# Weight pieces in self attention: the copies move to both ends of the row exponentials, the subtractions in among the row maxima

## The chip, the cores and the metric

One core of one Trainium2 chip runs the kernel. The metric is the device time of one execution in microseconds (us), smaller is better; the figure before is the median of three runs. Engines are named TensorE (PE; PEld is its weight load), VectorE (DVE), ScalarE (ACT), GpSimd (POOL) and SyncE (SP), which issues most of the transfers.

## The reference

A decoder layer on x of 4 x 512 x 512 numbers in fp32: causal self attention with 16 heads of 32 and rotary positions, cross attention to a masked context of 1601 rows, and a mixture of 16 experts (4 per token) beside a shared one, each followed by a residual and a layer norm.

```python
q, k, v = (proj(Wq), proj(Wk), proj(Wv))
q = q * cos + _rotate_half(q) * sin
k = k * cos + _rotate_half(k) * sin
att = jnp.einsum('bhqd,bhkd->bhqk', q, k) / math.sqrt(hd)
att = jax.nn.softmax(att + mask, axis=-1)
out = jnp.einsum('bhqk,bhkd->bhqd', att, v)
...
x = _layernorm(x + _L0_attn_ref(x, L0_attn_Wq, L0_attn_Wk, L0_attn_Wv, L0_attn_Wo), axis=-1)
x = _layernorm(x + _L0_xattn_ref(x, ctx_2048, mask_BxS2_bk0), axis=-1)
x = _layernorm(x + _L0_ffn_ref(x, ...), axis=-1)
```

## The kernel before

Products are made to fp32 accuracy from two parts of each operand: a high part in the multiplier's own format (fp32r) and the low rest, x - high. Three products of parts replace one. So every operand is split once: ScalarE copies it (the rounding copy is the high part), and VectorE or GpSimd subtracts that copy from the value.

Self attention (`self_attention`) works in 16 groups, numbered g = 0 to 15: four batches b of 512 rows, in each four groups hg of four heads. The engines run their own instruction streams and wait on semaphores. One group, in the order of TensorE's stream (`group` under `block.tensor`):

- Stage A: 16 tiles of row scores, n = 0 to 15 (L546, mask L548), in pairs, and between the pairs 40 of the 48 projection products (L506) of the next group. VectorE takes each tile's row maximum (L456), ScalarE its row exponentials with their sum (L331). A tile lies in one of three PSUM buffers, so the score of tile n waits for the exponential of tile n - 3. In groups with hg = 0, except the first, the output projection of the batch before (L525) and its residual follow.
- The row maxima are turned (L630), and ScalarE (L347) and VectorE (L471) copy them below q.
- Stage B: transposed scores (L562), their exponentials (L355) on ScalarE, the causal zeroing of diagonal blocks by GpSimd (`hide_later`, L263), and the products with v (L569). VectorE rotates q and k of the next group meanwhile (L391 to L409), ScalarE rounds q (`hi_q`, L303) and GpSimd takes its rest (`lo_q`, L252). GpSimd does `lo_q` behind the zeroing of the third block column, of four. `turn_heads` (L599) then transposes the heads of the next group, which waits for q's rest, the roped k and v; ScalarE (L323) and VectorE (L446) copy the result out, and the next group's scores begin.

Beside this, self attention splits the first 24 pieces of the experts' weights for the last part of the kernel. A piece is 128 x 512 numbers. It is fetched into one of two slots in a part of the buffer `rows` that is free till the end of the stage (`fetch`, L202), rounded by ScalarE (`hi_piece`, L314), its rest taken in place by VectorE (`lo_piece`, L427), and both parts are stored to memory (`store`, L207). A slot's fetch waits until the store of its piece before has landed. Groups 1 to 12 do two pieces each: k = 2(g - 1) and the next. Before the change ScalarE copies them behind the row exponentials n = 2 and n = 4, VectorE subtracts them both at the end of its part of the group, behind the copy of the turned inverses (`keep_inverse`, L417), and SyncE stores both and then fetches the next two. SyncE's stream also holds the loads of the next batch's x (`load_x`, L212).

Other work in the stages: in groups with hg = 3 ScalarE splits two blocks of x behind n = 1 and 3 (`hi_x`, L292), in groups with hg = 2 two behind n = 9 and 11, and GpSimd takes their rests (L247). Behind n = 6 ScalarE rounds the output of the group before (`hi_out`, L310), and GpSimd takes its rest (`lo_out`, L256). VectorE scales that output behind n = 3 (`finish_out`, L423).

Of the kernel before, what the change touches and what calls it, by code (L numbers as in the profile page):

```python
# [59 lines left out]
NF = 2  # L60
FIRST_GROUPS = range(1, 1 + FIRST * WE // FIRST_PIECE // NF)
# [12 lines left out]
def self_attention(nc, sem, rows, xT, x, wqkvT, woT, rope, w_experts, w_split, split_steps, gather_x1):  # L74
# [3 lines left out]
    with ExitStack() as ctx:  # L78
# [57 lines left out]
        def row_place(n):  # L136
            return score_ps[:, n % 3, :] if n % 3 < 2 else den_ps[:, :]
# [8 lines left out]
        def w_places(c):  # L146
            return staged[:, c * HG * GW:(c + 1) * HG * GW], wqkv[:, 0, c, :], wqkv[:, 1, c, :]

        def wo_places():
            return staged[:, DC * HG * GW:], *(wo[:, part, :, :].rearrange("p g n -> p (g n)") for part in range(2))  # L150
# [4 lines left out]
        def piece_place(k, part):  # L155

            at = (k % NF * 2 + part) * FIRST_PIECE
            return spare[:, at:at + FIRST_PIECE]

        def pieces_of(g):  # L160
            return range((g - 1) * NF, g * NF) if g in FIRST_GROUPS else range(0)

# [22 lines left out]
        with nc.Block() as block:  # L185

            @block.sync
            def _(sp):
                for c in range(DC):
                    sp.dma_start(x_raw[:, c, :], xT[0, :, c, :]).then_inc(chunk_in[c], 16)  # L190
                    sp.dma_start(w_places(c)[0], wqkvT[:, c, :]).then_inc(chunk_in[c], 16)
                sp.dma_start(cos_t[:, :, :], rope[0]).then_inc(tables_in, 16)
                sp.dma_start(sin_t[:, :, :], rope[1]).then_inc(tables_in, 16)
                sp.dma_start(wo_places()[0], woT).then_inc(wo_in, 16)
                def in_memory(k):
                    expert, at = k // (WE // FIRST_PIECE), k % (WE // FIRST_PIECE) * FIRST_PIECE
                    return w_experts[1 + expert, :, at:at + FIRST_PIECE], w_split[expert, :, :, at:at + FIRST_PIECE]

                def fetch(k):
                    if k >= NF:  # L200
                        sp.wait_ge(piece_out[k % NF], 16 * (k // NF))
                    sp.dma_start(piece_place(k, 1), in_memory(k)[0]).then_inc(piece_in[k % NF], 16)  # L202

                def store(k):
                    sp.wait_ge(piece_lo, k + 1)
                    at = k % NF * 2 * FIRST_PIECE
                    sp.dma_start(in_memory(k)[1], spare[:, at:at + 2 * FIRST_PIECE].rearrange("p (a n) -> p a n", a=2)  # L207
                                 ).then_inc(piece_out[k % NF], 16)

                def load_x(b):  # L210
                    sp.wait_ge(x_lo, b * TT)
                    sp.dma_start(x_raw[:, :, :], xT[b]).then_inc(x_in, 16)  # L212

                load_x(1)
                sp.wait_ge(w_lo, DC + 1)
                for k in range(NF):
                    fetch(k)
                sp.dma_start(rows[:, 0:NT - TT, :], x[:, 0:NT - TT, :]).then_inc(rows_in, 16)
                for g in FIRST_GROUPS:
                    if g % HG == 0 and g // HG + 1 < B:  # L220
                        load_x(g // HG + 1)
                    for k in pieces_of(g):
                        store(k)
                    for k in pieces_of(g + 1):
                        fetch(k)
                assert (B - 2) * HG in FIRST_GROUPS
                for slot in range(NF):
                    sp.wait_ge(piece_out[slot], 16 * len(FIRST_GROUPS))
                sp.dma_start(rows[:, NT - TT:NT, :], x[:, NT - TT:NT, :]).then_inc(rows_in, 16)
# [56 lines left out]
            def _(act):  # L286
# [25 lines left out]
                def hi_piece(k):  # L312
                    act.wait_ge(piece_in[k % NF], 16 * (k // NF + 1))
                    nc.scalar.activation(piece_place(k, 0).bitcast(F32R), piece_place(k, 1), ACT.Copy  # L314
                                         ).then_inc(piece_hi, 1)

                def group(b, hg, first, last):
                    g = b * HG + hg

                    act.wait_ge(scored_t, g * NS)  # L320
                    for h in range(GH):
                        act.wait_ge(turned, g * 2 * GH + 2 * h + 1)
                        nc.scalar.activation(q_st[0:3 * HD, h, :], proj_ps[0:3 * HD, 2 * h % 4, :],  # L323
                                             ACT.Copy).then_inc(q_stacked, 1)
                    for n in range(NS):
                        qt, h = n // GH, n % GH
                        w = (qt + 1) * P
                        act.wait_ge(maxed, g * NS + n + 1)
                        if n == 0:
                            act.wait_ge(inverted, g)  # L330
                        nc.scalar.activation(row_place(n)[:, 0:w], row_place(n)[:, 0:w], ACT.Exp,  # L331
                                             bias=neg_row_max[:, qt, h:h + 1], accum_out=row_sum[:, qt, h:h + 1]
                                             ).then_inc(row_exped, 1)
                        if n in (1, 3) and hg == HG - 1 and not last:
                            hi_x(b + 1, 2 + n // 2)
                        if n in (2, 4) and g in FIRST_GROUPS:
                            hi_piece(pieces_of(g)[n // 2 - 1])
                        if n == 6 and not first:
                            hi_out(g - 1, (hg - 1) % HG)
                        if n == 7 and g == 0:  # L340
                            hi_wo()
                        if n in (9, 11) and hg == HG - 2 and b < B - 1:
                            hi_x(b + 1, n // 2 - 4)

                    act.wait_ge(max_turned, g + 1)
                    for h in range(0, GH, 2):
                        nc.scalar.activation(q_st[3 * HD:P, h, :], den_ps[32 * h:32 * h + 32, :],  # L347
                                             ACT.Copy).then_inc(max_stacked_a, 1)
                    act.wait_ge(summed, g)
                    for kc in range(TT):  # L350
                        w = T - kc * P
                        for h in range(GH):
                            n = kc * GH + h
                            act.wait_ge(scored_t, g * NS + n + 1)
                            nc.scalar.activation(p_t[:, h, p_at[kc]:p_at[kc] + w],  # L355
                                                 score_ps[:, n % 2, kc * P:T], ACT.Exp).then_inc(exped, 1)
                            if n == 2 * GH + 1 and not last:
                                hi_q(g + 1)
# [11 lines left out]
            def _(dve):  # L370
# [48 lines left out]
                def finish_out(g):  # L419

                    dve.wait_ge(summed, g + 1)
                    dve.wait_ge(inv_kept, g + 1)
                    nc.vector.tensor_tensor(o_f[:, :], o_ps[:, :], o_f[:, :], ALU.mult).then_inc(o_scaled, 1)  # L423

                def lo_piece(k):
                    dve.wait_ge(piece_hi, k + 1)
                    nc.vector.tensor_tensor(piece_place(k, 1).bitcast(F32R), piece_place(k, 1), piece_place(k, 0),  # L427
                                            ALU.subtract).then_inc(piece_lo, 1)
# [11 lines left out]
                def group(b, hg, first, last):  # L440
                    g = b * HG + hg
# [7 lines left out]
                    for qt in range(TT):  # L449
                        for h in range(GH):  # L450
                            n = qt * GH + h
                            dve.wait_ge(scored, g * NS + n + 1)
                            if n == 0:
                                dve.wait_ge(max_lo, g)
                                dve.wait_ge(row_exped, g * NS)
                            nc.vector.tensor_reduce(neg_row_max[:, qt, h:h + 1], row_place(n)[:, 0:(qt + 1) * P],  # L456
                                                    AX, ALU.max, negate=True).then_inc(maxed, 1)
                            if n == 3 and not first:
                                finish_out(g - 1)
                    dve.wait_ge(maxed, g * NS + NS)  # L460
                    dve.wait_ge(max_turned, g)
                    nc.vector.tensor_copy(neg_max[:, :, :, 0], neg_row_max[:, :, :]).then_inc(max_hi, 1)
# [15 lines left out]
                    keep_inverse(g)  # L478
                    if g == 0:
                        lo_w(DC, wo_places())  # L480
                    for k in pieces_of(g):
                        lo_piece(k)

                dve.wait_ge(tables_in, 32)
                rotate(0)
# [1685 lines left out]
```

## Time and profile before

| | |
|---|---|
| median of 3 runs | 1492.63 us (1491.56 to 1495.46) |
| the profiled execution | 1484.37 us, span 1482.7 us, mean granted clock 0.947 |
| busy, TensorE / its weight loads | 1312.1 us (88%) / 1041.5 us (70%) |
| busy, VectorE / ScalarE / GpSimd | 839.9 (57%) / 709.2 (48%) / 390.8 (26%) us |
| self attention | about the first 520 us of the span |
| zeroing of diagonal blocks, L263, 256 times | 95.8 us busy |

The profile is of one execution, with every instruction's start and duration. A row of the timeline gives start, duration, engine, line of kernel.py, operation, written and read tensors and their shape; "xN" are N instructions merged; in brackets stand the engine's idle time just before and what ended it. Instructions of one engine can overlap a little, since the next is started before the last has drained.

### The profile page before, as it was taken

How to read it: one execution, taken by the hardware profiler on the slowest of the kernel's cores; microseconds unless marked ns; L12 is line 12 of the kernel's file. 1: busy time of each engine (PE TensorE's matmuls, PEld its weight loads, DVE VectorE, ACT ScalarE, POOL GpSimd, SP SyncE). 2: the span in 40 equal slices, each digit the busy share in tenths (PEclk: the TensorE clock that was granted, in tenths of full speed). 3: DMA queues.
4: the chain of work that ended last, by engine and by line, in shares of the span. 5: the costliest groups of instructions: out<-in, count | busy, mean ns of one | idle time of the engine just before them, and what ended most of it. 6: DMA issues, size and time to landing. Idle time of an engine off the chain costs nothing. (4 is left out here: it accounts for less than half of the span.)

```text
span 1482.7 us, 22215 instructions
## 1 busy us (share of the span) xinstructions
PE 1312.1 (88%) x7473; PEld 1041.5 (70%) x7473; DVE 839.9 (57%) x1764; ACT 709.2 (48%) x1589; POOL 390.8 (26%) x491
## 2 busy tenths in 40 slices
PE   5899999999999858999899997896999999899960
PEld 4666676666676447888788786785788887788850
DVE  6777677676766556665666655684333333233316
ACT  4777577577747624444344533422333333233323
POOL 0234223234322320100101000102454553555420
PEclk9999999999999879999999999998999999999985
DMA  4212111112110035677667574416888999985657
GB/s 184 100 44 89 54 58 43 72 44 84 46 57 1 1 129 195 214 241 264 221 224 256 186 252 147 187 61 241 287 200 269 272 229 316 276 205 109 108 92 298
DMA packets 96907, 235.59 MB, mean 159 GB/s; under 512 B 10584, under 2 KB 47452, under 8 KB 93856
## 3 DMA queue, kind: packets, MB, share of 16 engines
q1 hardware_dynamic: 78960, 188.96, 36.4%
q0 software_dynamic: 17840, 45.22, 14.8%
q8 instruction: 65, 1.06, 0.3%
q14 instruction: 42, 0.34, 0.1%
HBM read 146.20 MB, written 87.95 MB: 158 GB/s over the span
## 5 line engine op out<-in xcount | busy, mean ns | idle before, releaser
L1993 PE MATMUL e_both_ps<-e_w,e_x_t 128*128 x948 | 243.8, 406 | 9.3 <-DMA e_w<-w_split 9.3
L1993 PEld LDWEIGHTS e_both_ps<-e_w,e_x_t 128*128 128x128 f32 x948 | 174.6, 191 | 46.4 <-issue 9.7
L506 PE MATMUL proj_ps<-wqkv,x_sp 128*128 128x384 f32 x768 | 172.1, 354 | 10.8 <-DVE wqkv L378 10.8
L1860 POOL DMA_INDIRECT acc_rows<-e_y,token_row x79 | 125.4, 1587 | 174.7 <-ACT e_y L1904 85.6
L1173 PE MATMUL c_score_ps<-ct,x_t 128*128 128x402 f32 x768 | 160.8, 363 | 0.0
L263 POOL TENSOR_SCALAR_AFFINE_SELECT p_t<-p_t 128x128 f32<-128x128 f32 x256 | 95.8, 387 | 218.8 <-ACT p_t L355 215.0
L1196 PE MATMUL c_out_ps<-cr,weigh_t 128*128 128x512 f32 (+1 forms) x624 | 149.8, 397 | 1.4 <-DVE weigh_t L1014 1.4
L1173 PEld LDWEIGHTS c_score_ps<-ct,x_t 128*128 128x128 f32 x768 | 142.8, 196 | 5.6 <-issue 4.5
L506 PEld LDWEIGHTS proj_ps<-wqkv,x_sp 128*128 128x128 f32 x768 | 130.5, 193 | 12.6 <-issue 11.0
L1929 DVE TENSOR_TENSOR e_x_t<-e_turn_ps,e_x_t 128x512 fp32r<-128x512 f32 x79 | 54.6, 692 | 147.0 <-ACT e_x_t L1891 131.8
L1196 PEld LDWEIGHTS c_out_ps<-cr,weigh_t 128*128 128x128 f32 (+1 forms) x624 | 115.8, 188 | 28.7 <-issue 1.7
L2016 PE MATMUL e_down_ps<-e_w,e_h_t 128*128 x474 | 124.8, 398 | 7.1 <-DVE e_h_t L1941 7.1
L355 ACT ACTIVATE p_t<-score_ps 128x512 f32<-128x512 f32 (+3 forms) x256 | 101.7, 436 | 57.1 <-PE score_ps L562 54.0
L2016 PEld LDWEIGHTS e_down_ps<-e_w,e_h_t 128*128 128x128 f32 x474 | 89.4, 189 | 29.9 <-issue 8.6
L1897 ACT ACTIVATE e_gated<-e_both_ps 128x256 f32<-128x256 f32 x79 | 30.4, 385 | 166.5 <-PE e_both_ps L1993 162.5
L1851 POOL DMA_INDIRECT e_x_g<-x_rows,token_row x79 | 80.0, 1013 | 103.0 <-DVE token_row L1578 61.4
L1936 DVE TENSOR_TENSOR e_h_f<-e_both_ps,e_gated 128x256 f32<-128x256 f32 x79 | 33.5, 424 | 125.3 <-ACT e_gated L1897 123.9
L331 ACT ACTIVATE score_ps<-score_ps,neg_row_max 128x128 f32<-128x128 f32 (+3 forms) x176 | 87.3, 496 | 28.5 <-DVE neg_row_max L456 27.4
L456 DVE TENSOR_REDUCE neg_row_max<-score_ps 128x1 f32<-128x128 f32 (+3 forms) x176 | 82.6, 483 | 31.7 <-PE score_ps L548 30.1
L1904 ACT ACTIVATE e_y<-e_down_ps,e_weight 128x512 f32<-128x512 f32 x79 | 54.3, 688 | 95.2 <-PE e_down_ps L2016 81.1
L562 PE MATMUL score_ps<-q_st,k_st 128*128 128x256 f32 (+2 forms) x256 | 87.2, 400 | 13.7 <-ACT p_t L355 12.7
L562 PEld LDWEIGHTS score_ps<-q_st,k_st 128*128 128x128 f32 x256 | 43.3, 194 | 74.0 <-ACT p_t L355 48.8
(233 smaller groups left out, 2267.2 us busy)
## 6 DMA issues: line engine op xcount, KB each, us to landing
e_w<-w_split SPq DMA_DIRECT2D x15, 3072.0 KB, 12.1
w_split<-c_piece SPq DMA_DIRECT2D x96, 384.0 KB, 3.6
c_piece<-w_experts SPq DMA_DIRECT2D x96, 192.0 KB, 3.7
raw<-ctxT SPq DMA_DIRECT2D x16, 800.5 KB, 4.4
w_split<-rows SPq DMA_DIRECT2D x24, 512.0 KB, 3.5
raw<-ctx_rows SPq DMA_DIRECT2D x16, 768.0 KB, 5.3
acc_rows<-rows SPq DMA_DIRECT2D x8, 1024.0 KB, 12.0
rows<-w_experts SPq DMA_DIRECT2D x24, 256.0 KB, 2.8
```

The source lines that it names most:

```text
L263: nc.gpsimd.affine_select(out=block_of, in_=block_of, compare_op=ALU.is_ge, fill=0.0, base=0, pattern=[[1, P]], channel_multiplier=-1).the ...
L331: nc.scalar.activation(row_place(n)[:, 0:w], row_place(n)[:, 0:w], ACT.Exp, bias=neg_row_max[:, qt, h:h + 1], accum_out=row_sum[:, qt, h:h ...
L355: nc.scalar.activation(p_t[:, h, p_at[kc]:p_at[kc] + w], score_ps[:, n % 2, kc * P:T], ACT.Exp).then_inc(exped, 1)
L456: nc.vector.tensor_reduce(neg_row_max[:, qt, h:h + 1], row_place(n)[:, 0:(qt + 1) * P], AX, ALU.max, negate=True).then_inc(maxed, 1)
L506: mm = nc.tensor.matmul(proj_ps[:, tt, 0:GW], x_sp[:, xs, c, tt * P:(tt + 1) * P], wqkv[:, ws, c, hg * GW:(hg + 1) * GW], start=(c == 0 an ...
L562: nc.tensor.matmul(score_ps[:, n % 2, q0:T], k_st[:, h, kc * P:(kc + 1) * P], q_st[:, h, q0:T], start=True, stop=True).then_inc(scored_t, 1)
L1173: mm = nc.tensor.matmul(score_ps[:, f, 0:MQ], x1_t[:, xs, c, n % XR * P:(n % XR + 1) * P], ct[:, cs, c, f * MQ:(f + 1) * MQ], start=(late ...
L1196: mm = nc.tensor.matmul(out_ps[:, n % 2, :], weigh_t[0:k, ws, c, :], cr[0:k, cs, c, :], start=(c == 0 and m == 0), stop=(c == MC - 1 and m ...
L1851: nc.gpsimd.indirect_dma_start(x_g[:, m % XG, :], None, x2_rows, bass.IndirectOffsetOnAxis(ap=token_row[:, 0, m:m + 1], axis=0)).then_inc( ...
L1860: nc.gpsimd.indirect_dma_start(acc[m % 2], bass.IndirectOffsetOnAxis(ap=token_row[:, 1, m:m + 1], axis=0), y[:, m % YB, :], None, compute_ ...
L1993: mm = nc.tensor.matmul(both_ps[:, m % 2, :], x_t[:, m % 2, xs, c * P:(c + 1) * P], weights(slot, ws, c * GU, (c + 1) * GU), start=(c == 0 ...
L2016: mm = nc.tensor.matmul(down_ps[:, m % 2, :], h_t[:, m % 2, hs, i * P:(i + 1) * P], weights(slot, ws, DOWN + i * D, DOWN + (i + 1) * D), s ...
```

## The change

The first of a group's two pieces is rounded ahead of the first row exponential, the second behind the last. The rest of the first is taken behind the seventh row maximum (n = 6) of the same group, the rest of the second behind the second maximum (n = 1) of the next group. SyncE stores and fetches slot by slot. Nothing is computed otherwise.

```diff
@@ sync
                     for k in pieces_of(g):
                         store(k)
-                    for k in pieces_of(g + 1):
-                        fetch(k)
+                        if k + NF < n_pieces:
+                            fetch(k + NF)
@@ scalar, group
+                    for k in pieces_of(g)[0:1]:
+                        hi_piece(k)
                     for n in range(NS):
...
-                        if n in (2, 4) and g in FIRST_GROUPS:
-                            hi_piece(pieces_of(g)[n // 2 - 1])
...
+                    for k in pieces_of(g)[1:2]:
+                        hi_piece(k)
                     act.wait_ge(max_turned, g + 1)
@@ vector, group
+                            if n == 1:
+                                for k in pieces_of(g - 1)[1:2]:
+                                    lo_piece(k)
                             if n == 3 and not first:
                                 finish_out(g - 1)
+                            if n == 6:
+                                for k in pieces_of(g)[0:1]:
+                                    lo_piece(k)
...
-                    for k in pieces_of(g):
-                        lo_piece(k)
```

VectorE, from the end of group 2 into group 3, before:

```order
L409 TENSOR_TENSOR qk_sp<-qk_cos,qk_sp 128x16x32
L417 COPY o_f<-den_ps 128x512
L427 TENSOR_TENSOR rows<-rows 128x512 x2
L446 CAST k_st<-proj_ps 96x512 x4
L456 TENSOR_REDUCE neg_row_max<-score_ps 128x1 x2
L456 TENSOR_REDUCE neg_row_max<-den_ps 128x1
L456 TENSOR_REDUCE neg_row_max<-score_ps 128x1
L423 TENSOR_TENSOR o_f<-o_ps,o_f 128x512
L456 TENSOR_REDUCE neg_row_max<-score_ps 128x1
L456 TENSOR_REDUCE neg_row_max<-den_ps 128x1
L456 TENSOR_REDUCE neg_row_max<-score_ps 128x1 x2
```

The same stretch after the change (the subtraction is now L431, the maxima L460, the copy of k L450):

```order
L413 TENSOR_TENSOR qk_sp<-qk_cos,qk_sp 128x16x32
L421 COPY o_f<-den_ps 128x512
L450 CAST k_st<-proj_ps 96x512 x4
L460 TENSOR_REDUCE neg_row_max<-score_ps 128x1 x2
L431 TENSOR_TENSOR rows<-rows 128x512
L460 TENSOR_REDUCE neg_row_max<-den_ps 128x1
L460 TENSOR_REDUCE neg_row_max<-score_ps 128x1
L427 TENSOR_TENSOR o_f<-o_ps,o_f 128x512
L460 TENSOR_REDUCE neg_row_max<-score_ps 128x1
L460 TENSOR_REDUCE neg_row_max<-den_ps 128x1
L460 TENSOR_REDUCE neg_row_max<-score_ps 128x1
L431 TENSOR_TENSOR rows<-rows 128x512
```

The two subtractions have left the place behind the copy of the inverses and stand singly behind the second and the seventh maximum.

ScalarE, around the first row exponentials of group 1, before:

```order
L323 ACTIVATE q_st<-proj_ps 96x512 x4
L331 ACTIVATE score_ps,row_sum<-score_ps,neg_row_max 128x128 x2
L331 ACTIVATE den_ps,row_sum<-den_ps,neg_row_max 128x128
L314 ACTIVATE rows<-rows 128x512
L331 ACTIVATE score_ps,row_sum<-score_ps,neg_row_max 128x128
L331 ACTIVATE score_ps,row_sum<-score_ps,neg_row_max 128x256
L314 ACTIVATE rows<-rows 128x512
L331 ACTIVATE den_ps,row_sum<-den_ps,neg_row_max 128x256
```

And after the change (the piece's copy is L316, the exponentials L335):

```order
L325 ACTIVATE q_st<-proj_ps 96x512 x4
L316 ACTIVATE rows<-rows 128x512
L335 ACTIVATE score_ps,row_sum<-score_ps,neg_row_max 128x128 x2
L335 ACTIVATE den_ps,row_sum<-den_ps,neg_row_max 128x128
L335 ACTIVATE score_ps,row_sum<-score_ps,neg_row_max 128x128
L335 ACTIVATE score_ps,row_sum<-score_ps,neg_row_max 128x256
```

The first copy stands ahead of all exponentials; the second has moved out of this stretch, behind the last one and ahead of L351, the copy of the turned maxima.

## Rows read from the trace of the kernel before

**Rows 1.** The page: the span, and the engines' busy time.

```profile
span 1482.7 us, 22215 instructions
...
PE 1312.1 (88%) x7473; PEld 1041.5 (70%) x7473; DVE 839.9 (57%) x1764; ACT 709.2 (48%) x1589; POOL 390.8 (26%) x491
```

**Rows 2.** The timeline, stage B of group 2, some of its rows.

```profile
102.91 0.50 PE L630 MATMUL den_ps<-ident_r,neg_max 128*128 128x128 f32 x4
...
112.17 1.37 DVE L427 TENSOR_TENSOR rows<-rows 128x512 fp32r<-128x512 f32 x2
...
112.47 1.23 POOL L263 TENSOR_SCALAR_AFFINE_SELECT p_t<-p_t 128x128 f32<-128x128 f32 x2 [0.67 <-ACT p_t L355]
...
113.67 1.28 POOL L252 TENSOR_TENSOR qk_sp<-qk_cos,qk_sp 128x512 fp32r<-128x512 f32 x1
...
115.00 2.68 PE L599 MATMUL proj_ps<-ident_r,qk_sp 128*96 128x128 f32 x32 [0.17 <-POOL qk_sp L252]
...
115.86 2.54 DVE L446 CAST k_st<-proj_ps 96x512 fp32r<-96x512 f32 x4 [2.31 <-PE proj_ps L599]
...
117.96 0.39 PE L546 MATMUL score_ps<-k_st,q_st 96*128 96x256 f32 x1
```

**Rows 3.** The timeline, group 14, which has no pieces: first score to the next group's.

```profile
466.03 0.38 PE L546 MATMUL score_ps<-k_st,q_st 96*128 96x256 f32 x1
...
478.79 0.51 PE L630 MATMUL den_ps<-ident_r,neg_max 128*128 128x128 f32 x4
...
488.36 0.57 POOL L263 TENSOR_SCALAR_AFFINE_SELECT p_t<-p_t 128x128 f32<-128x128 f32 x2 [0.67 <-ACT p_t L355]
...
488.89 1.28 POOL L252 TENSOR_TENSOR qk_sp<-qk_cos,qk_sp 128x512 fp32r<-128x512 f32 x1
...
490.22 2.68 PE L599 MATMUL proj_ps<-ident_r,qk_sp 128*96 128x128 f32 x32 [0.17 <-POOL qk_sp L252]
...
493.19 0.38 PE L546 MATMUL score_ps<-k_st,q_st 96*128 96x256 f32 x1
```

**Rows 4.** The line L427: count, ns min/median/max, first and last start.

```profile
L427 DVE TENSOR_TENSOR rows<-rows x24: 674/724/772, 84.2 to 432.2; 128x512 fp32r<-128x512 f32 x24
```

**Rows 5.** The timeline of TensorE, ends of stage A in groups 1 and 3.

```profile
62.01 0.39 PE L546 MATMUL score_ps<-k_st,q_st 96*128 96x256 f32 x1
...
74.90 0.51 PE L630 MATMUL den_ps<-ident_r,neg_max 128*128 128x128 f32 x4
...
131.08 0.50 PE L630 MATMUL den_ps<-ident_r,neg_max 128*128 128x128 f32 x4
```

**Rows 6.** The timeline of VectorE, group 1: the third, seventh and eighth maximum.

```profile
63.89 0.29 DVE L456 TENSOR_REDUCE neg_row_max<-den_ps 128x1 f32<-128x128 f32 x1 [0.84 <-PE den_ps L548]
...
66.44 0.81 DVE L456 TENSOR_REDUCE neg_row_max<-score_ps 128x1 f32<-128x256 f32 x2 [0.43 <-PE score_ps L548]
```

**Rows 7.** The timeline of ScalarE, group 1: exponentials one and eight, a piece, the maxima.

```profile
62.84 0.34 ACT L331 ACTIVATE score_ps<-score_ps,neg_row_max 128x128 f32<-128x128 f32 x1 [0.74 <-DVE neg_row_max L456]
...
66.18 0.62 ACT L314 ACTIVATE rows<-rows 128x512 fp32r<-128x512 f32 x1
...
68.12 0.45 ACT L331 ACTIVATE score_ps<-score_ps,neg_row_max 128x256 f32<-128x256 f32 x1
...
75.45 1.20 ACT L347 ACTIVATE q_st<-den_ps 32x512 fp32r<-32x512 f32 x2 [0.69 <-PE den_ps L630]
```

**Rows 8.** The page's transfers: count, KB each, us from issue to landing.

```profile
w_split<-rows SPq DMA_DIRECT2D x24, 512.0 KB, 3.5
```

**Rows 9.** Busy time by window; the last numbers are granted clock, DMA share, GB/s.

```profile
143.30:146.70 3.40, 3.40 (x34) 3.26 (x33) 2.06 (x3) 2.17 (x5) 0.80 (x4) 0.50 0.79 270
```

**Rows 10.** The timeline of TensorE: the first score of group 4.

```profile
147.05 0.38 PE L546 MATMUL score_ps<-k_st,q_st 96*128 96x256 f32 x1
```

**Rows 11.** The timeline: VectorE beside L252 at the start, GpSimd in group 3.

```profile
24.41 1.75 DVE L398 TENSOR_TENSOR qk_cos<-qk_cos,qk_sin 128x512 f32<-128x512 f32 x1
...
122.09 1.28 POOL L247 TENSOR_TENSOR x_sp<-x_raw,x_sp 128x512 fp32r<-128x512 f32 x1 [0.61 <-ACT x_sp L292]
```

More of the change, by code:

```diff
@@ L158, in piece_place @@
             return spare[:, at:at + FIRST_PIECE]
+        n_pieces = NF * len(FIRST_GROUPS)
         def pieces_of(g):
```

## The prediction

> **What bounds the kernel now.** The page comes first: 1482.7 us of span, TensorE busy for 88% of it [rows 1]. The change touches only self attention, so the rest of the page is set aside, and the timeline of that stage is read group by group. Fourteen of its sixteen groups look alike. Stage A runs from the first row score (L546) to the transpose of the row maxima (L630); stage B from there to the next group's first row score. The other views needed are the timelines of VectorE, GpSimd and ScalarE around these marks.
>
> *Stage B.* In group 2 the transpose starts at 102.91 and the next group's first score at 117.96, 15.05 us later [rows 2]. The 32 turns of the heads (L599) cannot start before GpSimd has finished the low part of q (L252, 113.67 to 114.95); their row names it as releaser, and they start at 115.00. GpSimd is late because of the row before: two diagonal selects (L263) that take 1.23 us together, from 112.47, while VectorE runs the two piece subtractions (L427) from 112.17 for 1.37 us. Group 14 has no pieces [rows 3]: the same two selects take 0.57 us, L252 starts 10.10 us after the transpose and not 10.76, L599 11.43 and not 12.09, the next first score 14.40 and not 15.05. That is a control inside the trace: what differs there is the pair of pieces, and 0.65 us follows it. The subtractions are 24, two in each of groups 1 to 12, from 84.2 to 432.2 us [rows 4], and the slow pair of selects stands in each of these groups.
>
> *Stage A.* TensorE, VectorE and ScalarE form a ring: a score needs a free one of three buffers, a maximum needs its score, an exponential its maximum, and a score two places on needs that exponential. Group 1 with its pieces takes 74.90 - 62.01 = 12.89 us, group 14 without pieces 478.79 - 466.03 = 12.76 us [rows 2, 3, 5]. Group 3, where ScalarE also splits two blocks of x among its first four exponentials, takes 131.08 - 117.96 = 13.12 us [rows 2, 5]. So 1.24 us of piece work inside ScalarE's row exponentials costs 0.13 us of time, and 0.36 where the x splits are there too.
>
> **The change, part by part.**
>
> *The two subtractions leave the end of the group.* Twelve groups (1 to 12) issue two of them there. GpSimd's pair of selects falls back from 1.23 to 0.57 us, and L252, L599 and the next group come 0.65 us earlier: 12 x 0.65 = **7.8 us** gained, all on TensorE's path. Late next would be L252 itself behind its own selects; group 14 shows nothing else in the way. VectorE had 2.31 us of idle time before its next copy (L446) [rows 2], so its own saving there is worth nothing.
>
> *The second subtraction goes behind the second maximum of the next group.* VectorE idles 0.84 us there until the third score [rows 6]; one piece takes 0.72, at most 0.77 [rows 4]. It fits with some 0.1 us to spare. Cost 0; bound, if the slack is missed, a few hundredths per group.
>
> *The first subtraction goes behind the seventh maximum.* VectorE has no idle time between maxima seven and eight (0.81 us for both) [rows 6], so the eighth moves by 0.7 us: 66.44 + 0.42 + 0.72 + 0.42, about 67.95. Its exponential started at 68.12 in group 1 [rows 7], since ScalarE was behind with two pieces and the split of o; without the pieces ScalarE is free earlier, so this exponential starts near 68.0. The later maximum is paid for by ScalarE's lead. VectorE catches up where it now waits for the ninth score. Net: about 0.05 us faster than now.
>
> *ScalarE's first copy goes ahead of the first exponential.* ScalarE waits 0.74 us there for VectorE, and the copy (L314) takes 0.62 [rows 7]. Cost 0. The data must be there: pieces are fetched one at a time as their slot's store lands, 3.5 us after issue [rows 8]. The first slot is stored after the seventh maximum, more than 20 us before its next use; the second after the next group's second maximum, some 2 us into stage A, stored by 5.5 us, fetched (half the bytes, so at most another 3.5) by 9 us, and wanted at 12.7 (75.45 - 0.69 - 62.01).
>
> *ScalarE's second copy goes behind the last exponential.* ScalarE waits 0.69 us there for the transpose; 0.62 fits, with little to spare. TensorE's transpose waits for the last exponential, not for this copy. Cost 0, bound 0.1 us per group.
>
> *The DMA queue* alternates store and fetch instead of two and two. The transfers are the same 24 and 24. The loads of x for the next batch stand behind one more store and start some 10 us later in two groups; they are used two groups on. Cost 0.
>
> *Stage A in sum.* Bounded above by group 14's time in every group: 9 x 0.13 + 3 x 0.36 = 2.3 us gained. Bounded below by the piece behind the seventh maximum reaching TensorE whole: 12 x 0.72 = 8.6 us lost. I take the value near the upper bound, since ScalarE's lead covers the delay: 9 x 0.05 for groups like group 1, and 3 x 0.25 for groups 3, 7 and 11, which lose their backlog: **1.2 us** gained.
>
> *Sum:* 7.8 + 1.2 = 9.0 us. The profiled execution took 1484.37 us (span 1482.7), 8.3 us under the median 1492.63 of the runs shown; so I expect a span near 1473.7 and a median of 1492.63 - 9.0 = **1483.6 us**.
>
> **Clock.** TensorE's granted clock drops to half (1.2 GHz of its two levels, 2.4 and 1.2) during the turns of some groups, just after the stretch in which it waits for GpSimd [rows 9]. Group 3 is one; its stage B takes 147.05 - 131.08 = 15.97 us [rows 5, 10] against group 2's 15.05, so a drop costs 0.92 us. Among groups 1 to 12 seven have one (3, 5, 6, 7, 9, 10, 12). The waiting before the turns gets shorter, which should not bring more drops, but where they fall is not decided by this kernel alone: none would be another 6.4 us gained, all twelve 4.6 us lost. I leave seven in the sum and put this into the range.
>
> **A rule against the sum.** The rows show one engine standing still for the other: the pair of selects beside the pieces takes twice its usual time [rows 2, 3], and in the first group's start VectorE's L398, begun just behind L252, took 1.75 us [rows 11], some 1.0 more than the like subtractions of [rows 4]. The Trainium skill (SBUF — State Buffer, "SBUF: two separate sides") says that VectorE with two SBUF inputs and a GpSimd operation that reads SBUF exclude each other for a whole instruction, whichever starts first. The trace agrees in both directions. By that rule the moved subtraction can itself be blocked in stage A, by GpSimd's subtractions of 1.28 us; that is the first rival.
>
> **The rivals.**
>
> *1. The moved subtraction meets GpSimd's.* In group 3 the x subtraction (L247) starts at 122.09, 4.13 us after the first score [rows 2, 11]; the new piece would start at about 4.8. With ScalarE's piece gone, L247 starts some 0.5 us sooner and ends at about 4.9, so VectorE waits 0.1 us, in three groups only. At worst it waits L398's surplus of 1.0 us: 3 us, inside the range. GpSimd's split of o follows ScalarE's, which comes behind the seventh exponential, after the piece has ended (5.6 against 6.0). Were that one met in all twelve groups, 12 x 1.0 us come back: 1495.6 us, no change to be measured. Chance 0.04.
>
> *2. Nothing is freed.* Something else holds L599, and only stage A's 1.2 us is gained: 1491.4 us. For it: the turns also wait for roped k and for v. Against it: group 14, in full. Chance 0.04.
>
> *3. Slower: the ring of stage A takes both subtractions.* If neither the idle 0.84 us nor ScalarE's lead hides them, 12 x 1.44 = 17.3 us are added against 7.8 gained: 1492.6 + 9.5 = 1502.1 us. It decides from the point where more than 0.65 of the 1.44 us reach TensorE per group. For it: the last exponential ends the stage, and the ring is tight in its second half. Against it: 1.24 us on ScalarE cost only 0.13 in the same ring. Chance 0.03.
>
> *4. More: the clock.* With the shorter wait no turn falls to half clock: 9.0 + 6.4 gained, 1477.2 us. Chance 0.05.
>
> **How the numbers follow.** The forecast has 0.84. Its own range goes from 1483.6 - 1.1 (stage A at its bound) - 3.7 (four drops fewer) = 1478.8 to 1483.6 + 4.6 (five more) = 1488.2; rounded out, 1478.5 to 1488.5. Left out are rivals 1, 2 and 3 (0.11), rival 4 (0.05) and the forecast's tails (0.04). About 0.3% (4.5 us) is what a measurement of this kernel can tell from no change: faster is forecast and rival 4, 0.89; same is rivals 1 and 2, 0.08; slower 0.03.
>
> **What would show it.** Right: the two selects before L252 take about 0.57 us in all groups; L252 starts 10.1 us and the next first score 14.4 us after L630 where the clock is full; stage A takes 12.8 to 12.9 us, in group 3 too; no idle time of ScalarE on the fetched piece. Wrong: stage A over 13.1 us, with VectorE late at the ninth maximum and TensorE waiting for an exponential at the tenth to twelfth score; a piece subtraction of well over 0.77 us (blocked by GpSimd); L347 starting later than 0.55 us after L630; or L599 still at 12.1 us.

## The result, and the profile after

| | before | after |
|---|---|---|
| median of the runs | 1493.97 us (4 runs, 1491.56 to 1495.46) | 1472.51 us (4 runs, 1466.78 to 1475.8) |
| ratio, 95% interval | | 0.9849 (0.9815 to 0.9884) |
| the same comparison again, 6 runs of after, 23 of before | 1490.98 us | 1474.62 us, 0.9874 (0.9848 to 0.9901) |
| span of the profiled execution | 1482.7 us | 1474.1 us |

Faster, and by about twice the 9.0 us of the forecast: 18.8 us by the ratio of the second comparison (14.8 to 22.7). The ratio is not that of the two medians, which lie 21.5 us apart in the first comparison and 16.4 in the second. The spans of the two profiles differ by only 8.6 us, so where the time went has to be read by stage. The mark used from here on is a group's first row score. In the profile before, groups 1 and 15 begin at 62.01 and 493.19, 431.18 us apart; in the one after:

```profile
63.90 0.38 PE L554 MATMUL score_ps<-k_st,q_st 96*128 96x256 f32 x1
...
478.54 0.39 PE L554 MATMUL score_ps<-k_st,q_st 96*128 96x256 f32 x1
```

That is 414.64 us, **16.5 us less**. The rest of the difference lies where the change touches nothing. Group 1 begins 1.9 us later, though group 0 has no pieces; 0.7 of it is in stage B of group 0 (17.68 us, and 17.01 before), where the stretch at half clock is 6.8 us long and was 3.4. In the eleven other profiles of this study that mark lies between 61.96 and 64.34, and neither end belongs to one kernel: filler, with the old code in group 0, has 63.67, both_at_seven, with the new, 62.21. From group 15 to the end the profile before takes 989.5 us, the one after 995.6; the code there is the same in all kernels, and the thirteen profiles give 989.5 to 999.4. The profile before is the luckiest of them. 16.5 - 1.9 - 6.1 = 8.6.

**Stage B.** The timeline of group 2 after, rows that answer to [rows 2]; its transpose of the maxima starts at 103.79 (the maxima are now L460, the pieces' subtraction L431, their copy L316, the selects L265, q's rest L254, the turns L607):

```profile
103.79 0.43 PE L638 MATMUL den_ps<-ident_r,neg_max 128*128 128x128 f32 x3
...
113.35 0.57 POOL L265 TENSOR_SCALAR_AFFINE_SELECT p_t<-p_t 128x128 f32<-128x128 f32 x2 [0.66 <-ACT p_t L359]
...
113.89 1.28 POOL L254 TENSOR_TENSOR qk_sp<-qk_cos,qk_sp 128x512 fp32r<-128x512 f32 x1
...
115.22 2.67 PE L607 MATMUL proj_ps<-ident_r,qk_sp 128*96 128x128 f32 x32 [0.17 <-POOL qk_sp L254]
...
118.17 0.38 PE L554 MATMUL score_ps<-k_st,q_st 96*128 96x256 f32 x1
```

The pair of selects is back at 0.57 us; q's rest starts 10.10 us after the transpose, and the next group 14.38 us after it. Stage B reads 14.37 to 14.41 us in all groups from 1 to 13: each is what group 14 was before [rows 3].

**Stage A.** VectorE in group 3, after, to be read against [rows 6]:

```profile
118.66 0.54 DVE L460 TENSOR_REDUCE neg_row_max<-score_ps 128x1 f32<-128x128 f32 x2
119.12 0.68 DVE L431 TENSOR_TENSOR rows<-rows 128x512 fp32r<-128x512 f32 x1
120.03 0.29 DVE L460 TENSOR_REDUCE neg_row_max<-den_ps 128x1 f32<-128x128 f32 x1 [0.23 <-PE den_ps L556]
...
122.59 0.42 DVE L460 TENSOR_REDUCE neg_row_max<-score_ps 128x1 f32<-128x256 f32 x1 [0.44 <-PE score_ps L556]
122.93 0.68 DVE L431 TENSOR_TENSOR rows<-rows 128x512 fp32r<-128x512 f32 x1
123.53 0.42 DVE L460 TENSOR_REDUCE neg_row_max<-score_ps 128x1 f32<-128x256 f32 x1
```

One subtraction stands in the idle stretch before the third maximum, which has shrunk to 0.23 us from the 0.84 read in group 1 before; the other moves the eighth maximum to 123.53. ScalarE at the end of the same stage, against [rows 7]:

```profile
130.66 0.62 ACT L316 ACTIVATE rows<-rows 128x512 fp32r<-128x512 f32 x1
131.44 1.20 ACT L351 ACTIVATE q_st<-den_ps 32x512 fp32r<-32x512 f32 x2 [0.16 <-PE den_ps L638]
```

The copy fills the wait for the transpose, 0.16 us of it are left, and L351 starts 0.54 us after the transpose (130.90), as before. Stage A takes 12.74, 12.77, 12.73 and 24.04 us in groups 1 to 4, where it took 12.89, 12.95, 13.12 and 24.16: as little as in groups without pieces. Over the twelve groups that is 2.4 us.

**The clock.** Windows, one over each of groups 5 and 6. The columns are busy time and instructions of TensorE, its weight loads, VectorE, ScalarE and GpSimd; then granted clock, DMA share and GB/s. Before:

```profile
186.00:215.00 29.00, 27.04 (x205) 19.30 (x204) 20.85 (x40) 21.51 (x59) 8.55 (x18) 0.94 0.18 61
215.00:244.00 29.00, 27.27 (x204) 19.20 (x197) 20.57 (x39) 22.00 (x60) 11.14 (x20) 0.94 0.16 54
```

And after:

```profile
184.00:211.00 27.00, 25.64 (x197) 18.14 (x196) 20.16 (x39) 21.16 (x59) 7.87 (x18) 1.00 0.16 59
211.00:239.00 28.00, 26.73 (x203) 19.08 (x204) 21.04 (x42) 22.62 (x62) 10.40 (x20) 1.00 0.17 58
```

Before, each has a stretch at half clock around its turns; after, none, nor has any other group from 1 to 13. Group 14, which had none before, has one after:

```profile
473.50:476.70 3.20, 3.20 (x26) 2.35 (x26) 0.39 (x1) 1.50 (x6) 2.25 (x5) 0.50 0.00 0
```

So the 16.5 us are 12 x 0.66 = 7.9 (stage B at full clock), 2.4 (stage A) and 6.2, which is 431.18 - 414.64 less the other two. The last is the half clock: what stage B takes beyond its time at full clock adds up to 6.0 us in seven of groups 1 to 12 before, 0.8 in group 13 before, and 0.8 in group 14 after.

### The profile page after: what moved, and what is told of

Read it like the earlier page. It is cut to its first block and busy times, and to the rows that moved or that the text cites. A ratio compares the mean times of both kernels' runs of the same rounds, so it can differ in the third digit from the quotient of the medians.

```text
span 1474.1 us, 22215 instructions
## 1 busy us (share of the span) xinstructions
PE 1308.5 (89%) x7473; PEld 1039.5 (71%) x7473; DVE 837.3 (57%) x1764; ACT 710.4 (48%) x1589; POOL 381.9 (26%) x491
## 5 line engine op out<-in xcount | busy, mean ns | idle before, releaser
L1181 PE MATMUL c_score_ps<-ct,x_t 128*128 128x402 f32 x768 | 163.8, 368 | 0.0
L1181 PEld LDWEIGHTS c_score_ps<-ct,x_t 128*128 128x128 f32 x768 | 145.8, 200 | 5.7 <-issue 4.5
L265 POOL TENSOR_SCALAR_AFFINE_SELECT p_t<-p_t 128x128 f32<-128x128 f32 x256 | 87.3, 353 | 220.3 <-ACT p_t L359 216.4
L335 ACT ACTIVATE score_ps<-score_ps,neg_row_max 128x128 f32<-128x128 f32 (+3 forms) x176 | 86.7, 493 | 29.0 <-DVE neg_row_max L460 28.2
L460 DVE TENSOR_REDUCE neg_row_max<-score_ps 128x1 f32<-128x128 f32 (+3 forms) x176 | 83.0, 483 | 29.1 <-PE score_ps L556 27.4
L570 PE MATMUL score_ps<-q_st,k_st 128*128 128x256 f32 (+2 forms) x256 | 86.6, 398 | 13.7 <-ACT p_t L359 12.6
```

What stands on the lines that cost most here:

```text
L265: nc.gpsimd.affine_select(out=block_of, in_=block_of, compare_op=ALU.is_ge, fill=0.0, base=0, pattern=[[1, P]], channel_multiplier=-1).the ...
L570: nc.tensor.matmul(score_ps[:, n % 2, q0:T], k_st[:, h, kc * P:(kc + 1) * P], q_st[:, h, q0:T], start=True, stop=True).then_inc(scored_t, 1)
L1181: mm = nc.tensor.matmul(score_ps[:, f, 0:MQ], x1_t[:, xs, c, n % XR * P:(n % XR + 1) * P], ct[:, cs, c, f * MQ:(f + 1) * MQ], start=(late ...
```

## The experiments

One table for all of them. "A" is stage A of groups 1, 2 and 3; "B" stage B at full clock in groups 1 to 12; "half" the number of groups 1 to 13 with a half-clock stretch in or just ahead of the turns; "late" how many of these begin 10.6 us or more after the transpose of the maxima; "1 to 15" the time between the first scores of groups 1 and 15. All five are from the one profiled execution, and the ratio is of timed runs to the kernel before on the same chip.

| kernel | A | B | half | late | 1 to 15 | median us | ratio (95%) |
|---|---|---|---|---|---|---|---|
| before | 12.89 12.95 13.12 | 15.06 | 8 | 7 | 431.18 | 1493.97 | |
| before, again | 12.87 12.93 13.11 | 15.06 | 7 | 6 | 431.04 | 1491.60 | 0.9996 (0.9973 to 1.0018) |
| after | 12.74 12.77 12.73 | 14.39 | 0 | 0 | 414.64 | 1472.51 | 0.9849 (0.9815 to 0.9884) |
| after, again | 12.73 12.80 12.74 | 14.40 | 1 | 0 | 414.69 | 1474.62 | 0.9874 (0.9848 to 0.9901) |
| subs_only | 12.87 17.50 18.75 | 14.40 | 2 | 0 | 478.56 | 1537.93 | 1.0305 (1.0279 to 1.0331) |
| copies_only | 12.76 12.80 13.12 | 15.06 | 3 | 2 | 427.70 | 1489.18 | 0.9997 (0.9977 to 1.0018) |
| subs_same_group | 12.90 13.14 13.13 | 14.40 | 1 | 0 | 417.86 | 1479.16 | 0.9910 (0.9882 to 0.9938) |
| both_at_seven | 12.73 13.27 13.22 | 14.40 | 2 | 0 | 420.74 | 1483.17 | 0.9940 (0.9916 to 0.9964) |
| late_q | 12.82 12.79 12.74 | 14.86 | 2 | 2 | 421.32 | 1481.88 | 0.9933 (0.9906 to 0.9961) |
| late_q3 | 12.75 12.78 12.77 | 15.10 | 6 | 5 | 428.16 | 1487.77 | 0.9982 (0.9954 to 1.0009) |
| late_q3_filler | 12.75 12.78 12.76 | 15.09 | 2 | 0 | 424.38 | 1484.20 | 0.9953 (0.9926 to 0.9981) |
| filler | 13.08 12.95 13.11 | 15.06 | 1 | 0 | 425.30 | 1486.68 | 0.9976 (0.9955 to 0.9997) |
| a_filler | 12.75 12.78 12.74 | 14.65 | 0 | 0 | 417.50 | 1477.78 | 0.9922 (0.9888 to 0.9956) |

**The two kernels again.**

> The kernel before, unchanged, beside itself. Theory 1 (the clock in self attention): its profile shows six to ten of the fourteen full groups with a half-clock stretch in the turns, not always the same ones, and its median is 1489 to 1496 us. Rival (chance in the later stages): the number of half-clock groups stays seven or eight, and the executions differ by what happens after the first 620 us. Ratio to itself 1.000 within 0.002 in both cases.

> The changed kernel, unchanged. Theory 1: again no or at most two half-clock stretches in groups 1 to 13, group 15's first score again near 478.5 us, and a time 1.2 to 1.6% below the kernel before. Rival: half-clock stretches come back in five or more groups, and group 15's first score lies at 482 us or later.

The changed kernel does as its theory 1 has it: only group 13 has a half-clock stretch, and the time is 1.26% below. The kernel before does not separate its two: seven half-clock groups (3, 5, 6, 7, 8, 9, 11) lie in the range of theory 1, and are also what the rival named. The time between groups 1 and 15 repeats within 0.2 us in each kernel, though the groups that lose their clock are in part others. The 12 runs of before beside itself lie between 1481.44 and 1498.22 us. Such a spread was not seen in self attention, where the two profiles of each kernel agree; the 989.5 to 999.4 us of the later part speak for the rival. One run of the 12 was profiled, so this is not shown.

**Only the subtractions.** From the changed kernel:

```diff
-                    for k in pieces_of(g)[0:1]:
-                        hi_piece(k)
                     for n in range(NS):
...
+                        if n in (2, 4) and g in FIRST_GROUPS:
+                            hi_piece(pieces_of(g)[n // 2 - 1])
...
-                    for k in pieces_of(g)[1:2]:
-                        hi_piece(k)
```

> Only the subtractions moved; ScalarE's copies stay behind the exponentials n = 2 and 4. Theory 1: stage B 14.4 us as in the changed kernel, stage A 12.9 to 13.3 us (the second subtraction no longer covered by ScalarE's lead), so period 27.3 to 27.6 us, and 1476 to 1482 us. Rival (the copies make the gain): 1488 us or more.

Both expectations were wrong: 3% slower than before. ScalarE's waits in the window of self attention name it, and its timeline in group 2:

```profile
ACT rows L316 <- DMA rows<-w_experts: 39.0, 11, 4.5
```

```profile
96.66 0.63 ACT L316 ACTIVATE rows<-rows 128x512 fp32r<-128x512 f32 x1 [3.17 <-DMA rows<-w_experts]
```

The second piece of a group is subtracted behind the next group's second maximum. Its slot is stored and fetched again only then, and the copy behind n = 4 stands waiting for it, with eleven exponentials behind it in ScalarE's queue. TensorE in turn stands idle once for 2.85 to 4.38 us in stage A of each of groups 2 to 12, and each has a half-clock stretch that begins in this wait or within 1.5 us of its end; these are not in the table's count. The late subtraction needs the late copy. I had worked out this deadline for the change (some 9 us into the stage) and not for the experiment.

**Only the copies.** Both subtractions back at the end of the group:

```diff
-                            if n == 1:
-                                for k in pieces_of(g - 1)[1:2]:
-                                    lo_piece(k)
...
-                            if n == 6:
-                                for k in pieces_of(g)[0:1]:
-                                    lo_piece(k)
...
+                    for k in pieces_of(g):
+                        lo_piece(k)
```

> Only ScalarE's copies moved; both subtractions stay at the end of the group. Theory 1: the pair of selects again 1.23 us, stage B 15.05 us at full clock, stage A 12.75 us, half-clock stretches in five or more groups, 1487 to 1492 us. Rival (the copies make the gain): 1480 us or less.

No gain that can be measured, as expected, and stage B is the old one:

```profile
84.86 1.24 POOL L265 TENSOR_SCALAR_AFFINE_SELECT p_t<-p_t 128x128 f32<-128x128 f32 x2 [0.66 <-ACT p_t L359]
86.07 1.26 POOL L254 TENSOR_TENSOR qk_sp<-qk_cos,qk_sp 128x512 fp32r<-128x512 f32 x1
```

Two things differ from what was expected. Stage A is 12.76 us only in group 1: from group 2 on a copy often finds its piece not there (0.31 us in group 2, ahead of the first exponential). ScalarE's waits for fetched pieces add up to 6.7 us, in nine waits. So each half of the change misses a deadline without the other: the early copy needs the early subtraction too. And there were three half-clock groups, not five or more, although TensorE waited for GpSimd just as long as before, 7.7 us in twelve waits. Theory 1 failed in this point; it is taken up below.

**The subtractions alone, with no deadline missed.** Copies at n = 2 and 4, as in subs_only, and both subtractions in the same group. VectorE's part, from the changed kernel:

```diff
-                            if n == 1:
-                                for k in pieces_of(g - 1)[1:2]:
-                                    lo_piece(k)
...
-                            if n == 6:
-                                for k in pieces_of(g)[0:1]:
+                            if n in (6, 10):
+                                for k in pieces_of(g)[n // 10:n // 10 + 1]:
                                     lo_piece(k)
```

> ScalarE's copies back behind n = 2 and 4, both subtractions in the same group, behind the maxima n = 6 and 10, so that no fetch comes late. Theory 1 (what the subtractions held up is GpSimd; what they cost among the maxima is small): stage B 14.4 us, ScalarE waits for no fetched piece, stage A 12.9 to 13.2 us in groups 1 and 2, no or few half-clock stretches, 1474 to 1480 us. Rival (the move of the copies is what pays, beyond the deadline of the fetch): stage A 13.5 us or more, and 1482 us or more.

As theory 1 has it: ratio 0.9910, stage B 14.40 us, one half-clock group. Most of the gain comes from taking VectorE's subtractions away from GpSimd's selects. What the copies' places add is in stage A: 417.86 - 414.67 = 3.2 us between this kernel and the changed one (the mean of its two profiles). In group 3 it also shows rival 1's collision, on VectorE and on GpSimd:

```profile
123.65 1.17 DVE L429 TENSOR_TENSOR rows<-rows 128x512 fp32r<-128x512 f32 x1
```

```profile
122.99 1.28 POOL L249 TENSOR_TENSOR x_sp<-x_raw,x_sp 128x512 fp32r<-128x512 f32 x1 [0.59 <-ACT x_sp L294]
```

Started 0.66 us into GpSimd's subtraction of x, VectorE's takes 1.17 us where 0.68 is its time alone. In the changed kernel the longest of the 24 takes 0.684 us:

```profile
L431 DVE TENSOR_TENSOR rows<-rows x24: 680/681/684, 68.7 to 424.4; 128x512 fp32r<-128x512 f32 x24
```

There the second x subtraction of group 3 ends at 123.04, 0.11 us after the piece's has begun (122.93), since without ScalarE's piece it comes earlier; nothing of a wait is seen.

```profile
120.39 2.65 POOL L249 TENSOR_TENSOR x_sp<-x_raw,x_sp 128x512 fp32r<-128x512 f32 x2 [4.25 <-ACT x_sp L294]
```

Both cases fit a wait that ends some 0.12 us before GpSimd's end in the profile: in subs_same_group that end is at 124.27, 0.62 us after VectorE's start, and the piece was 0.49 us longer. This is an estimate from two instances.

**Both subtractions behind the seventh maximum.**

```diff
-                            if n == 1:
-                                for k in pieces_of(g - 1)[1:2]:
-                                    lo_piece(k)
...
-                                for k in pieces_of(g)[0:1]:
+                                for k in [*pieces_of(g - 1)[1:2], *pieces_of(g)[0:1]]:
```

> The changed kernel with the second piece's subtraction moved from behind the next group's second maximum to behind its seventh, where now two stand in a row, 1.4 us. Theory 1 (one subtraction there is covered by ScalarE's lead, a second is not): stage A 13.2 to 13.6 us from group 2 on, 12 x 0.5 to 12 x 0.8 = 6 to 10 us slower than the changed kernel. Rival (the ring of stage A has room for both): stage A 12.8 us, the changed kernel's time. A fetch that lands too late for the second copy would show as ScalarE waiting for the piece.

Stage A is 13.22 to 13.28 us from group 2 on, 0.5 more than in the changed kernel. The time between groups 1 and 15 is 6 us longer (420.74 against 414.67), 5.2 of it in stage A and the rest one half-clock stretch more; the medians, 1483.17 and 1474.62, were not measured side by side. One subtraction there is covered, a second is not. ScalarE shows it in group 3, at the eighth exponential:

```profile
123.43 0.45 ACT L335 ACTIVATE score_ps<-score_ps,neg_row_max 128x256 f32<-128x256 f32 x1 [0.45 <-DVE neg_row_max L460]
```

**What brings the half clock.** Two edits. The first makes GpSimd late in the changed kernel with no VectorE work beside it (two selects, then three in late_q3):

```diff
                         pool.wait_ge(exped, g * GH * TT + kc * GH + h + 1)
+                        if kc == 2 and h == 2 and g in FIRST_GROUPS:
+                            pool.wait_ge(padded, 2 * (g - 1))
+                            for i in range(2):
+                                nc.gpsimd.affine_select(out=pad[:, i, :], in_=ident_f[:, :], compare_op=ALU.is_ge,
+                                                        fill=0.0, base=0, pattern=[[1, P]], channel_multiplier=-1
+                                                        ).then_inc(padded, 1)
```

The second gives TensorE something to do while it waits for GpSimd, in the kernel before (filler), in late_q3, and in all groups but the last of the changed one (a_filler):

```diff
                         scores_t(g, kc, 0)
+                        if kc == 3 and g in FIRST_GROUPS:
+                            pe.wait_ge(roped, g * 6 + 11)
+                            pe.wait_ge(v_copied, g + 2)
+                            for _ in range(3):
+                                nc.tensor.matmul(proj_ps[:, 0, :], k_st[:, 0, 0:P], q_st[:, 0, :],
+                                                 start=True, stop=True)
                         values(g, hg, kc - 1)
```

> The changed kernel, and in groups 1 to 12 GpSimd does two further selects of 0.29 us on a spare tile before the third select of the third block column, which makes the rest of q about 0.6 us late without any VectorE work beside it. Theory 1 (GpSimd's lateness sets both the 0.65 us and the half clock): L599 starts 12.0 us after the transpose of the maxima, stage B takes 15.0 us at full clock, half-clock stretches are back in four to nine of groups 1 to 13, and the time is 1485 to 1491 us. Rival (the clock is a matter of VectorE's work, or of the length of the period alone and chance): stage B 15.0 us, but no more than two half-clock stretches, 1481 to 1484 us.

> The kernel before, and in groups 1 to 12 TensorE does three further products of 512 columns, written to a buffer that the turns overwrite, while it waits for GpSimd before the third product with v. Theory 1 (idle time of TensorE ahead of the turns is what brings the half clock): stage B stays 15.05 us or up to 0.15 longer, half-clock stretches in no more than two of groups 1 to 13, group 1 to group 15 about 425 us (431 before), 1484 to 1488 us. Rival (the half clock follows the phase of the period, whatever TensorE does): six to nine stretches, 431 us or more, 1490 us or more.

late_q came out as its rival has it, with two half-clock groups and 1481.88 us. It is a weak test, since q's rest was 0.47 us late and not 0.6, and TensorE's wait 0.44 us and not 0.64. filler decides. Its stage B is to 0.01 us that of the kernel before, its half-clock groups went from eight to one (13, which has no filler), and groups 1 to 15 take 425.30 us against 431.18. So it is not GpSimd's lateness that brings the half clock, but TensorE's idle time in it. The timed gain is small, 0.9976 with 0.9997 as upper end, 3.6 us of 1490: less than the 5.9 us of the profile, but within its interval.

> As late_q, with three further selects of 0.29 us, so that the rest of q is about 0.77 us late, as late as in the kernel before, with no VectorE work beside it. Theory 2 (after late_q and filler: half-clock stretches come where TensorE idles long enough ahead of the turns; 0.48 us of lateness brought two): stage B 15.1 us at full clock, four or more half-clock stretches in groups 1 to 13, group 1 to group 15 at 426 to 431 us, time 1486 to 1491 us. Rival (chance): no more than two stretches again, 1482 to 1485 us.

> late_q3 with filler's three further products of TensorE before the third product with v. Theory 2: the same stage B of 15.1 us, but at most one half-clock stretch in groups 1 to 12, so group 1 to group 15 at 423 to 424 us, and 3 us or more below late_q3. Rival (the half clock does not follow TensorE's idle time): as many stretches as late_q3, and its time.

> The changed kernel with the three further products in groups 0 to 14. Theory 2: the wait before the third product with v has shrunk to about 0, so the products delay stage B by up to 0.5 us per group, up to 7 us in all, and they can save at most the one half-clock stretch that the changed kernel shows in groups 13 or 14 (0.8 us) and the one in group 0: 1475 to 1481 us, no better than the changed kernel. Rival (the filler pays anyway through the clock): 1470 us or less.

With three selects the rest of q is as late as in the kernel before, and six groups lose their clock (1, 2, 5, 6, 9 and 11). That nearly restores the old time (0.9982) with every piece in its new place. With the filler on top stage B stays at 15.09 us and two groups lose theirs, where at most one was expected; 3.8 us between groups 1 and 15 come back. TensorE's waits in self attention say what the filler took away. late_q3:

```profile
PE o_ps L585 <- POOL p_t L273: 8.1, 12, 0.7
```

The kernel before has the same row, 7.7 us in twelve waits. In the views of after, filler and late_q3_filler there is no such row: the wait was removed in one and filled in the two others. In the changed kernel itself the filler can only cost: stage B 14.65 us and not 14.39, 417.50 us between groups 1 and 15, and no half-clock stretch in groups 0 to 14. It gains nothing where that wait is gone. No variant beat the changed kernel.

The profiles say one thing more when each stretch is timed from the transpose of the maxima. In groups 1 to 13 there are two kinds. One begins 9.9 to 10.1 us after it, before TensorE's wait for GpSimd has begun (that wait ends at 10.7 to 10.9 us). There are at most two of it per profile, in kernels with the wait and without it: group 13 before, group 13 of after, again, and both groups of late_q3_filler are of this kind, and so is group 14 of after. The other begins 10.6 to 12.6 us after it, inside the wait or behind it. All 22 of these ("late" in the table) are in the five profiles whose kernels have the wait, none in the eight others, and the seven that the prediction counted are among them. So the wait is needed for this kind. It is not enough: with the same wait copies_only has two, the kernel before seven and six. What decides which groups lose their clock, and what brings the first kind, stays open; each variant was profiled once.

## Why the prediction was wrong

**Stage B, 7.8 us: right,** in mechanism and size. 7.9 us are read, q's rest at 10.10 and the next score at 14.39 us, from group 14's rows. late_q3 shows from the other side that GpSimd's lateness alone makes the 15.1 us. Rival 2 falls.

**The slack of the moved pieces: right.** The copy ahead of the first exponential and the subtraction behind the second maximum fit. In group 1 the eighth exponential started 5.88 us after the first score (69.78 - 63.90), where 6.0 was worked out and 6.11 stood before. The fetches came in time, in the pair. Rival 3 falls: no more than a few hundredths of the 1.44 us can have reached TensorE, and both_at_seven shows where it begins, with a second subtraction in the same place.

**Stage A, 1.2 us: mis-sized.** It is 2.4 us, the upper bound given (2.3) and a little more: groups 1 to 4 gain 0.15, 0.18, 0.39 and 0.12 us, and groups 5 to 12 about the same again. The estimate kept back some 0.1 us per group for the delayed maximum; there was nothing to keep.

**The clock: the step that failed.** "I leave seven in the sum and put this into the range." Seven half-clock stretches among groups 1 to 12 were counted, at 0.92 us each, and the text even noted that they come just after TensorE's wait for GpSimd, and that the wait would shrink. It then treated their number as chance, put the wait's effect on them at nothing, kept all seven in the sum, and gave 0.05 to the case that they vanish. In groups 1 to 12 they all vanished, in both profiles of the changed kernel, and filler, which moves nothing, shows that they go with the wait. They were worth 6.0 us, 0.86 each. With them and stage A's bound the sum would have been 7.8 + 2.3 + 6.4 = 16.5 us, which is what self attention gave. That it agrees to a tenth is partly luck: 6.4 is a little too much, and 0.8 gained in group 13 and 0.8 lost in group 14 cancel.

**The rule and rival 1: the mechanism is there, the wait was not.** In group 3 the piece started at 4.76 us and the x subtraction ended at 4.87, where 4.8 and 4.9 were worked out. The 0.1 us that VectorE was to wait there is not seen. subs_same_group shows the wait that the Trainium skill describes (SBUF — State Buffer, "SBUF: two separate sides"): 0.49 us longer. The trace agrees with the rule there. In the changed kernel the two overlap by 0.11 us in the profile, and none of the 24 subtractions is lengthened.

**The range.** It left room for four half-clock stretches fewer, though the text had named the case of seven fewer, so the 1472.51 us, and the 1474.62 of the second comparison, lie below it. The second comparison's interval, 14.8 to 22.7 us, holds the 16.5 us of self attention. The first one's, 17.3 to 27.6 us, begins just above it. Whether some 2 us more were gained outside self attention, or whether the runs of these two comparisons drew well, was not settled: the later part's time varies by 10 us between profiles of the same code.

## What to carry to other kernels

An engine that works on SBUF (the core's working memory) beside another can delay it without any semaphore between them: compare the same instruction in a repetition where the neighbour is absent, which here gave stage B's gain per group to 0.01 us before the move was made. When a wait of TensorE is followed by a stretch at half clock, ask whether the stretch is part of the wait's price. Here it was: the stretches that began in or behind the wait went when it was removed, and when it was filled. And where pieces circulate through a few slots, moving one step alone can miss a fetch: here the copies alone gained nothing that could be measured, and the subtractions alone lost 3%.

## What the runs showed of the hardware that was not expected

- A wait of TensorE of 0.44 to 0.69 us per group, shortly ahead of the transposes, went with stretches at 1.2 GHz in place of 2.4 that began in it or behind it: seven and six in the two profiles of the kernel before, five in late_q3, two in late_q (the 0.44 us) and two in copies_only, none in the eight profiles in which the wait was removed or filled. Three further products in the wait did no useful work and still saved 3.8 and 5.9 us between groups 1 and 15.
- A second kind of half-clock stretch, up to two per profile, began 9.9 to 10.1 us into stage B, where TensorE had waited there no longer than 0.41 us at a time; no run says what brings it.
- VectorE's subtraction with both inputs in SBUF took 1.17 us beside GpSimd's, against 0.68 alone, and two selects of GpSimd 1.23 beside two of VectorE's, against 0.57.
- The part of the kernel that no variant touched took 989.5 to 999.4 us in thirteen profiles. A single pair of profiles said 8.6 us where self attention had gained 16.5.
